# Routed experts on one core: parts of 16, 24 and 24 tiles, token rows scattered at other places, tile tables built sooner

## The chip, the core and the metric

One core of one Trainium2 chip runs the whole program. The metric is the device time of one execution in microseconds (us). TensorE (PE) multiplies and transposes, VectorE (DVE) and ScalarE (ACT) work on elements, GpSimd (POOL) does the same more slowly and issues the DMAs that need computed row numbers or an addition, and SyncE (SP) issues the plain DMAs.

## The reference

Tensors are float32. The input is 4 sequences of 2048 tokens with 256 channels, 8192 tokens in all.

```python
h = layernorm(x) * (1 + ca) + sa
x = x + ga * attention(h)            # 16 heads of 16, causal
h = layernorm(x) * (1 + cb) + sb
logits = h @ gate_w.T + bias         # 12 experts: 8 with weights, 4 that return h
top_w  = softmax(top 2 logits)
for e in the two chosen:
    y_e = silu(h @ w1[e].T) @ w2[e].T        # w1[e] 512 x 256, w2[e] 256 x 512
ffn = sum of top_w * y_e over chosen e < 8, plus (sum of top_w over chosen e >= 8) * h
x = x + gb * ffn
```

A token is computed only by the experts that it chose.

## The kernel before, in words

The program has three stages: attention, routing (`route`) and the experts (`experts`). The change touches the last two, and the sizes of buffers that attention clears.

**Parts.** The 64 tiles of 128 tokens are cut into three parts, `PARTS`. For each part there is a buffer `slot_x{p}` in HBM in which the rows of one expert lie together, each expert's rows rounded up to whole tiles of 128. A row holds the 256 channels of the normalised token and 6 numbers beside them (its place in `out`, its first expert, its two weights).

**Routing** runs over 16 blocks of 4 tiles as a hand-written pipeline. `blocks` (L1240) calls, in step s, each listed stage for block s - lag. DVE adds the attention output to `x` and takes the statistics (`residual`), ACT normalises into `hn`, POOL multiplies `hn` into `h2s` (`modulate`, L1734), DVE adds the shift into `h2` (`shifted`, L1600), PE transposes it and computes the logits, and DVE picks the two largest (`top2`). When all blocks of a part are through, DVE builds the one-hot choice (`chosen`, L1278 to L1285), PE counts with two matmuls (`counts`, L1319 and L1320), and DVE turns the counts into the row number of each token and choice (`placed`, first instruction L1327). Parts 0 and 2 have the lags 5 and 6, part 1 has lags of its own. After the pipeline DVE builds a table for each part (`tile_table`, L1360 to L1368): which expert each tile of the slot buffer belongs to (`eid`, `eidf`), where it changes (`turn`), and how many pairs of tiles there are (`npair`). The table uses the buffer of `hn` as scratch.

The pipeline also loads and transposes the weights of the 8 experts. `w_in` has two buffers for each of the two matrices; PE transposes each matrix in two halves (L1578), so 32 halves, each of which increments `wt_done`, and ACT copies them away. SP loads the next matrix (L1396, L1399) when a buffer has been transposed.

**Scatter.** `scatter_row` (L1376) is one indirect DMA on POOL: 128 rows of `h2` to their places in `slot_x{p}`, for one tile and one of its two choices, 134 KB. A tile has two of them, and a row DMA of a tile waits until that of three tiles earlier has landed. Part 0 is scattered during routing: three row DMAs in each of the last 8 blocks, the other 8 behind them. Parts 1 and 2 are scattered during the experts of the part before.

**Experts** go part by part, and in a part by pairs of tiles. For a tile, SP loads its 128 slots into `xs` (L1844), PE transposes it (L1870), multiplies with `w1` (L1878) and with `w2` (L1887), ACT copies `x_t` (L1919) and that expert's `w1` (L1923) and applies silu (L1915), DVE multiplies with the token's weight into `ys` (L1978, a ring of four buffers), and POOL adds it into `out` by an indirect DMA with addition (L2005). The buffer `ys[t % 4]` may be written again when the add of tile t - 4 has landed. An add waits for the add two tiles earlier, and where the expert changes (`turn`) for the one just before it, since the same token can be in both.

POOL's order in part p is written out (L2008 to L2026): pair i's two adds, then row DMAs of the next part until `due(p, i)` tiles are scattered, then in some pairs a zero term. A zero term (L1764 on DVE, the names `wc` and `zb` are one buffer; L1773 on POOL) adds the share of the four experts that return their input, for one group of four tiles; there are 16, and `ZTERMS` says in which part. SP may load the first tile of the next part once POOL has seen all its rows land and has incremented `x_ready`; this is checked once per pair, behind its adds.

Of the kernel before, what the change touches and what calls it, by code (L numbers as in the profile page):

```python
# [38 lines left out]
NB = NTOK // BLK  # L39
# [12 lines left out]
E, EZ, F = 8, 4, 512  # L52
# [3 lines left out]

PARTS = [16, 20, 28]
FIRST = [sum(PARTS[:p]) for p in range(len(PARTS))]
# [4 lines left out]
SCATTERING = 8  # L63
AHEAD = 0
NFILL = 12
# [6 lines left out]
GROUPS_OF = [list(range(FIRST[p] // TPB, (FIRST[p] + PARTS[p]) // TPB)) for p in range(NPARTS)]  # L72
ZTERMS = [GROUPS_OF[2], GROUPS_OF[0], GROUPS_OF[1]]
part_of = [p for p, n in enumerate(PARTS) for _ in range(n)]
XB = 4
# [1304 lines left out]
def scatter_tile(pool, d, r, t, scat):  # L1380

    for c in range(2):
        scatter_row(pool, d, r, t, c, scat)
# [37 lines left out]
def route(nc, a, d, k, r, w, w_in, w_ld, ps, out, scat, first, retired):  # L1421
    with ExitStack() as ctx:
# [35 lines left out]
        LASTS = [(FIRST[p] + PARTS[p]) // TPB - 1 for p in range(NPARTS)]  # L1458
        bank = ps[:, 7, :]

        with nc.Block() as block:
# [58 lines left out]
            def _(pe):  # L1520
# [60 lines left out]

                blocks((6, counts(0, 2)), (10, counts(1)), (0, output), (3, logits), (8, weights(0, 1)), (2, normed), (8, weights(1, E)))

            @block.vector
            def _(dve):
# [87 lines left out]
                def zeros(t):  # L1673
                    if t == LASTS[0]:
                        chains[0].zero_weights(dve, s, r)

                dve.memset(r["h2"][:, :, C:CE], 0.0).then_inc(ext_zero, 1)
                dve.wait_ge(ext_zero, 1)
                blocks((2, scales), (3, shifted), (5, top2), (0, attended), (1, residual), (4, inverses), (4, table),
                       (5, chosen(0, 2)), (6, placed(0, 2)), (7, zeros), (9, chosen(1)), (11, placed(1)))  # L1680
                dve.wait_ge(topi_done, NB)
                dve.wait_ge(mult_done, NB)
                for p in range(NPARTS):
                    tile_table(dve, s, r, p, cmp, eidf, last, turned)

            @block.scalar
            def _(act):
# [36 lines left out]

                blocks((1, deviation), (1, normalise), (5, shares(0, 2)), (10, shares(1)), (2, normed), (8, weights))

            @block.gpsimd
            def _(pool):
                def modulate(t):
                    pool.wait_ge(hn_done, t + 1)  # L1730
                    if t >= 1:
                        pool.wait_ge(mod_done, t)
                    apart(pool)
                    pool.tensor_tensor(h2s[:, :, :], hn[:, :, :], wide(k["sbc"][:, t // BPS, 1, None, :], 1, TPB), ALU.mult).then_inc(mult_done, 1)  # L1734

                todo = [(t, c) for t in range(PARTS[0] + AHEAD) for c in range(2)]

                def scatter():
                    t, c = todo.pop(0)
                    if (t, c) == (PARTS[0], 0):  # L1740
                        pool.wait_ge(pos_done, 4)
                    scatter_row(pool, d, r, t, c, scat[part_of[t]])

                def scatters(t):
                    if t >= NB - SCATTERING:
                        pool.wait_ge(pos_done, 2)
                        pool.wait_ge(mult_done, t + 1)
                        for _ in range(3):
                            scatter()

                blocks((0, modulate), (0, scatters))
                while todo:
                    scatter()
                scattered(pool, 0, scat[0])
# [21 lines left out]
def experts(nc, d, k, r, w, zb, ps, out, scat):  # L1776
# [3 lines left out]
    with ExitStack() as ctx:  # L1780
# [26 lines left out]
        ov = out.rearrange("b (n j p) c -> (b n) p j c", p=P, j=TPB)  # L1807
        later = [range(FIRST[p + 1] + (AHEAD if p == 0 else 0), FIRST[p + 1] + PARTS[p + 1]) if p + 1 < NPARTS else range(0) for p in range(NPARTS)]

        def due(p, i):  # L1810
            return len(later[p]) if i == NPAIR[p] - 1 else min(len(later[p]), -(-(i + 1) * len(later[p]) * 10 // (NPAIR[p] * 7)))

# [22 lines left out]
        with nc.Block() as block:  # L1835
# [157 lines left out]
            def _(pool):  # L1993
                for p in range(NPARTS):
                    def body(t, q, i):
                        pool.wait_ge(y_done[p], t + 1 + 2)
                        if t > 1:
                            pool.wait_ge(add_done[p][q], 16 * i)
                        if t in (1, 2):
                            pool.wait_ge(add_done[p][1 - q], 16)  # L2000
                        if t > 2:
                            turn = pool.value_load(r["turn"][0:1, p, t:t + 1], min_val=0, max_val=16)  # L2002
                            pool.wait_ge(add_done[p][1 - q], turn + 16 * ((t - 1) // 2))
                        apart(pool)
                        pool.indirect_dma_start(rows, bass.IndirectOffsetOnAxis(ap=idx[:, p, t:t + 1], axis=0), ys[:, t % YR, :], None,  # L2005
                                                compute_op=ALU.add).then_inc(add_done[p][q], 16)

                    used = tiles_used(pool, p)  # L2008
                    n, told = 0, not later[p]
                    for i in range(NPAIR[p]):  # L2010
                        pair(pool, i, used, body)
# [62 lines left out]
```

## Time and profile before

| | |
|---|---|
| median of 3 runs (lowest to highest) | 2663.47 us (2662.32 to 2663.79) |
| the profiled execution: time, and the span of its instructions | 2661.45 us, 2659.7 us |
| instructions | 48344 |
| PE busy, share of the span | 2484.9 us, 93% |
| DVE | 1904.5 us, 72% |
| ACT | 1668.7 us, 63% |
| POOL | 769.8 us, 29% |
| attention ends, routing begins | about 1970 us |
| experts begin | 2127.68 us |

Times in the rows below are microseconds from the start of the span. Busy time of an engine is time within its instructions; waiting, register and branch instructions are not in it. For an indirect DMA the record on POOL is the time in which POOL makes its descriptors, not that of the transfer. A bracket at the end of a row, `[2.10 <-PE ps L1887]`, is the idle time of that engine before the instruction, and what ended it.

### The profile page before, as it was taken

Reading aid. Unit: us, or ns where it says so; the run is one execution under the profiler, and the core shown is the slowest. Engines: PE = TensorE matmul, PEld = TensorE weight load, DVE = VectorE, ACT = ScalarE, POOL = GpSimd, SP = SyncE. Lnnn points to the kernel's source line nnn. Section 1 sums busy time; section 2 is a strip of 40 time slices with the busy share of each in tenths; the row PEclk is TensorE's granted clock in tenths of the full one; section 3 lists DMA queues with packets and bytes.
Section 4 is the critical chain, followed back from the end, with each engine's and each line's share of the span. In section 5 each row is a group of like instructions: output and inputs, shape, how many; then the busy total and the mean of one; then the engine's idle time right before and its main releaser. Section 6 shows DMA issues by size and latency. Waiting matters only on the chain. (4 is left out here: it accounts for less than half of the span.)

```text
span 2659.7 us, 48344 instructions
## 1 busy us (share of the span) xinstructions
PE 2484.9 (93%) x16082; PEld 1284.4 (48%) x16083; DVE 1904.5 (72%) x3227; ACT 1668.7 (63%) x2986; POOL 769.8 (29%) x895
## 2 busy tenths in 40 slices
PE   6987889999999999999999999999988798788998
PEld 3554233333333333333333333333347687678997
DVE  5987768788788788787787887887638644444654
ACT  2666357777777777777777777777764454344554
POOL 2545201121121111111111111111215467676443
PEclk8998789999999999999999999999999799899999
DMA  5798643252342442432432432320247656665653
GB/s 177 206 250 225 124 78 89 64 117 86 88 91 84 93 92 83 93 92 79 97 92 75 99 82 58 74 59 20 68 131 228 212 118 125 113 123 102 98 80 60
DMA packets 226331, 287.43 MB, mean 108 GB/s; under 512 B 29494, under 2 KB 179798, under 8 KB 225750
## 3 DMA queue, kind: packets, MB, share of 16 engines
q1 hardware_dynamic: 186988, 237.28, 35.1%
q0 software_dynamic: 32016, 41.44, 9.2%
q10 hardware_dynamic: 7136, 6.32, 0.7%
q8 instruction: 101, 1.65, 0.3%
q14 instruction: 90, 0.74, 0.1%
HBM read 143.51 MB, written 140.55 MB: 107 GB/s over the span
## 5 line engine op out<-in xcount | busy, mean ns | idle before, releaser
L238 DVE TENSOR_REDUCE mxc<-ps 128x2 f32<-128x1024 f32 (+4 forms) x1168 | 1298.1, 1149 | 316.0 <-PE ps L226 165.8
L1186 ACT ACTIVATE probs<-ps 128x512 f32<-128x512 f32 (+1 forms) x2240 | 1177.5, 587 | 462.0 <-PE ps L1143 450.4
L1159 PE MATMUL ps<-probs,vs 128*32 128x512 f32 (+3 forms) x5120 | 599.6, 541 | 1.3 <-POOL probs L1076 1.2
L1143 PE MATMUL ps<-qs,ks 99*128 99x512 bf16 (+3 forms) x1760 | 504.3, 352 | 13.9 <-DMA qs<-m_t 9.1
L226 PE MATMUL ps<-ks,qs 96*128 96x512 bf16 (+3 forms) x1760 | 464.4, 354 | 25.2 <-DVE mxc L238 17.4
L1076 POOL TENSOR_SCALAR_AFFINE_SELECT probs<-probs 128x512 f32<-128x512 f32 x256 | 162.4, 637 | 868.5 <-ACT probs L1186 868.4
L1143 PEld LDWEIGHTS ps<-qs,ks 99*128 99x128 bf16 x1760 | 147.5, 97 | 380.1 <-ACT probs L1186 271.8
L1878 PE MATMUL ps<-x_t,w_at 128*128 128x128 f32 x1984 | 250.1, 280 | 7.8 <-ACT w_at L1923 5.9
L2005 POOL DMA_INDIRECT out<-ys,idx x121 | 194.5, 1607 | 209.7 <-DMA out<-ys,idx 115.1
L226 PEld LDWEIGHTS ps<-ks,qs 96*128 96x128 bf16 x1760 | 163.4, 99 | 178.8 <-DVE mxc L238 42.4
L1878 PEld LDWEIGHTS ps<-x_t,w_at 128*128 128x128 f32 x1984 | 238.2, 196 | 10.3 <-ACT w_at L1923 7.9
L1887 PE MATMUL ps<-w2t,hid_t 128*128 x968 | 231.0, 382 | 6.8 <-ACT hid_t L1915 4.8
L1143 PE MATMUL ps<-shared 99*128 99x512 bf16 (+3 forms) x800 | 228.4, 349 | 0.0
L1159 PEld LDWEIGHTS ps<-probs,vs 128*32 128x32 f32 x5120 | 100.9, 108 | 228.8 <-issue 119.2
L226 PE MATMUL ps<-shared 96*128 96x512 bf16 (+3 forms) x800 | 207.8, 349 | 2.0 <-DVE mxc L238 1.8
L1978 DVE TENSOR_TENSOR ys<-ps,gm 128x256 f32<-128x256 f32 x121 | 51.4, 425 | 214.8 <-PE ps L1887 121.9
L1887 PEld LDWEIGHTS ps<-w2t,hid_t 128*128 128x128 f32 x968 | 175.4, 191 | 27.3 <-issue 8.2
L1923 ACT COPY w_at<-shared 128x1024 f32 x127 | 132.9, 1046 | 62.8 <-issue 56.2
L1919 ACT COPY x_t<-ps 128x256 f32<-128x256 f32 x127 | 47.2, 372 | 159.6 <-PE ps L1870 114.0
L1060 POOL CAST mparts<-negm 128x16 bf16<-128x16 f32 x64 | 12.6, 198 | 461.9 <-DVE negm L1205 461.9
L1143 PEld LDWEIGHTS ps<-shared 99*128 99x128 bf16 x800 | 66.9, 96 | 163.7 <-ACT probs L1186 118.2
L1376 POOL DMA_INDIRECT slot_x<-h,pos x128 | 132.1, 1032 | 43.0 <-issue 37.1
(172 smaller groups left out, 2220.5 us busy)
## 6 DMA issues: line engine op xcount, KB each, us to landing
ks<-k_parts SPq DMA_DIRECT2D x66, 256.0 KB, 4.1
qs<-q_parts SPq DMA_DIRECT2D x66, 256.0 KB, 4.1
xs<-slot_x SPq DMA_DIRECT2D x127, 131.0 KB
v_ones<-vout SPq DMA_DIRECT2D x64, 256.0 KB, 3.6
vs<-v_ones SPq DMA_DIRECT2D x64, 256.0 KB, 3.2
attn_t<-o_sb SPq DMA_DIRECT2D x64, 256.0 KB, 2.7
slot_x<-zero SPq DMA_DIRECT2D x36, 393.0 KB, 3.0
q_parts<-parts SPq DMA_DIRECT2D x96, 128.0 KB, 2.7
```

Source lines behind the costliest of these rows:

```text
L226: ins = pe.matmul(o[:, h, :], qs[0:SROWS, h0 + h, i * P:(i + 1) * P], ks[0:SROWS, h0 + h, 512 * c:512 * c + w], start=first, stop=not diag ...
L238: return dve.tensor_reduce(mxc[:, h0:h0 + nh, i, c], unit_view(ps, u, at), AX_X, ALU.max)
L1076: pool.affine_select(at, at, pattern=[[0, HG], [1, P]], base=0, channel_multiplier=-1, compare_op=ALU.is_ge, fill=keep).then_inc(mask_done, 1)
L1143: ins = pe.matmul(o[:, h, :], ks[r][0:SROWS + MROWS, h0 + h, j * P:(j + 1) * P], qs[r][0:SROWS + MROWS, h0 + h, J * QJ + lo:(J + 1) * QJ], ...
L1159: ins = pe.matmul(o_ps[SLOT * g:SLOT * (g + 1), lo:QJ], vs[:, r, j, SLOT * g:SLOT * (g + 1)], probs[:, (NKT * r + m) % NPB, g, 0:QJ - lo], ...
L1186: act.activation(probs[:, (NKT * r + m) % NPB, h0:h0 + nh, 0:QJ - lo], st_view(r, s), ACT.Exp, scale=DH ** -0.5).then_inc(exp_done, 1)
L1376: pool.indirect_dma_start(d[f"slot_x{p}"][:, :], bass.IndirectOffsetOnAxis(ap=r["pos"][c][:, t:t + 1], axis=0), r["h2"][:, t, :], None).th ...
L1878: ins = pe.matmul(ph[:, q, f * P:(f + 1) * P], w1_at[:, q, c, f * P:(f + 1) * P], x_t[:, q, c, :], start=(c == 0), stop=(c == KC - 1))
L1887: ins = pe.matmul(py[:, q, 0:C], h_t[:, q, f, :], w["w2t"][:, bass.ds(e, 1), f, :].rearrange("p o c -> p (o c)"), start=(f == 0), stop=(f ...
L1923: act.copy(w1_at[:, q, :, :], w["w1t"][:, bass.ds(e, 1), :, :].rearrange("p o c f -> p (o c) f")).then_inc(w1_done[p], 1)
L1978: dve.tensor_tensor(ys[:, t % YR, :], py[:, q, 0:C], gm[:, t % YR, :], ALU.mult).then_inc(y_done[p], 1)
L2005: pool.indirect_dma_start(rows, bass.IndirectOffsetOnAxis(ap=idx[:, p, t:t + 1], axis=0), ys[:, t % YR, :], None, compute_op=ALU.add).then ...
```

## The change

It cuts the parts otherwise, 16, 24 and 24 tiles in place of 16, 20 and 28. In routing, each of the last 8 blocks carries two row DMAs in place of three; of the other 16, the n-th (from 0) waits until 2n + 2 halves of weights are transposed. DVE builds the table of part 0 in step 17, that of part 1 in step 20, right behind `chosen` of part 2, and only that of part 2 at the end. In the experts, POOL scatters six tiles of part 1 (12 row DMAs) ahead of the first add, and the due times of the others follow another formula. Of the 16 zero terms, 2, 4 and 10 stand in the three parts, where it was 7, 4 and 5. The value of `turn` is loaded ahead of the waits of its add. `AT` makes the lags of part 1 follow from its last block; the steps come out as before (17, 18 and 19).

```diff
-PARTS = [16, 20, 28]
+PARTS = [16, 24, 24]
...
-AHEAD = 0
+EARLY = 6
...
-ZTERMS = [GROUPS_OF[2], GROUPS_OF[0], GROUPS_OF[1]]
+ZTERMS = [GROUPS_OF[2][:2], GROUPS_OF[2][2:], GROUPS_OF[0] + GROUPS_OF[1]]
...
+        AT = NB + 1 - LASTS[1]
...
-                blocks((6, counts(0, 2)), (10, counts(1)), (0, output), (3, logits), (8, weights(0, 1)), (2, normed), (8, weights(1, E)))
+                blocks((6, counts(0, 2)), (AT + 1, counts(1)), (0, output), (3, logits), (8, weights(0, 1)), (2, normed), (8, weights(1, E)))
...
+                def tables(p):
+                    def stage(t):
+                        if t == LASTS[p + 1]:
+                            dve.wait_ge(mult_done, NB)
+                            tile_table(dve, s, r, p, cmp, eidf, last, turned)
+                    return stage
+
...
-                       (5, chosen(0, 2)), (6, placed(0, 2)), (7, zeros), (9, chosen(1)), (11, placed(1)))
-                dve.wait_ge(topi_done, NB)
-                dve.wait_ge(mult_done, NB)
-                for p in range(NPARTS):
-                    tile_table(dve, s, r, p, cmp, eidf, last, turned)
+                       (5, chosen(0, 2)), (5, tables(1)), (6, placed(0, 2)), (7, zeros), (AT, chosen(1)),
+                       (AT, tables(0)), (AT + 2, placed(1)))
+                tile_table(dve, s, r, NPARTS - 1, cmp, eidf, last, turned)
...
                         pool.wait_ge(mult_done, t + 1)
-                        for _ in range(3):
+                        for _ in range(2):
                             scatter()
 
                 blocks((0, modulate), (0, scatters))
-                while todo:
+                for n in range(len(todo)):
+                    pool.wait_ge(wt_done, 2 * n + 2)
                     scatter()
                 scattered(pool, 0, scat[0])
...
         def due(p, i):
-            return len(later[p]) if i == NPAIR[p] - 1 else min(len(later[p]), -(-(i + 1) * len(later[p]) * 10 // (NPAIR[p] * 7)))
+            early = EARLY if p == 0 else 0
+            return min(len(later[p]), early - (-(i + 1) * (len(later[p]) - early) * 20 // (NPAIR[p] * 13)))
...
                     def body(t, q, i):
+                        if t > 2:
+                            turn = pool.value_load(r["turn"][0:1, p, t:t + 1], min_val=0, max_val=16)
                         pool.wait_ge(y_done[p], t + 1 + 2)
...
                         if t > 2:
-                            turn = pool.value_load(r["turn"][0:1, p, t:t + 1], min_val=0, max_val=16)
                             pool.wait_ge(add_done[p][1 - q], turn + 16 * ((t - 1) // 2))
...
                     n, told = 0, not later[p]
+                    if p == 0:
+                        while n < EARLY:
+                            scatter_tile(pool, d, r, later[0][n], scat[1])
+                            n += 1
```

POOL from the last block of routing to the first adds of the experts, before (`h2s` is the product of `modulate`, L1376 a row DMA, L2005 an add, L1773 a zero term):

```order
L1734 TENSOR_TENSOR h2s<-hn,sbc 128x1024
L1376 DMA slot_x<-h,pos 16640x262 x11
L1461 UNCONDITIONAL_BRANCH
L1992 UNCONDITIONAL_BRANCH
L1823 TENSOR_LOAD npair
L1823 ISA x2
L1823 TENSOR_LOAD npair
L1823 ISA x2
L1827 COMPARE_AND_BRANCH
L2005 DMA out<-ys,idx 8192x256
```

and now:

```order
L1740 TENSOR_TENSOR h2s<-hn,sbc 128x1024
L1376 DMA slot_x<-h,pos 15616x262 x18
L1462 UNCONDITIONAL_BRANCH
L1998 UNCONDITIONAL_BRANCH
L1829 TENSOR_LOAD npair
L1829 ISA x2
L1829 TENSOR_LOAD npair
L1829 ISA x2
L1376 DMA slot_x<-h,pos 15616x262 x12
L1833 COMPARE_AND_BRANCH
L2012 DMA out<-ys,idx 8192x256
```

Behind the last product stand 18 row DMAs in place of 11, the last 16 with waits for `wt_done`, and 12 more stand between the experts' begin and the first add.

DVE between the choice of part 2 (L1285) and its ranks (L1327), before:

```order
L1280 MEMSET c_flags 128x8
L1282 TENSOR_TENSOR c_oh<-c_idxf,iota_e 128x336 x2
L1285 TENSOR_TENSOR c_ohs<-c_oh 128x28x8
L1327 SCALAR_TENSOR_TENSOR c_cum<-c_flags,ps 128x224
L1328 TENSOR_SCALAR c_cnt_i<-c_cum 128x8
```

and now:

```order
L1285 TENSOR_TENSOR c_ohs<-c_oh 128x24x8
L1360 TENSOR_SCALAR last<-tend 128x1 x2
L1361 TENSOR_TENSOR hn<-tend,iota_t 128x464
L1362 CAST npair<-last 128x2
L1363 TENSOR_REDUCE eidf_all<-hn 128x58
L1364 TENSOR_SCALAR npair<-npair 128x2
L1365 TENSOR_TENSOR turned_at<-eidf_all 128x57
L1366 TENSOR_SCALAR turn<-turned_at 128x57
L1367 TENSOR_SCALAR eidf<-eidf_all 128x58
L1368 CAST eid<-eidf 128x58
L1327 SCALAR_TENSOR_TENSOR c_cum<-c_flags,ps 128x192
```

The table of part 1 has moved from behind everything to this place; that of part 0 stands the same way behind the choice of part 1.

## Rows read from the trace of the kernel before

**Rows 1.** Windows: us, busy of PE, PEld, DVE, ACT, POOL (instructions), PEclk, DMA share, GB/s

```profile
2131.00:2278.00 147.00, 123.31 (x831) 112.52 (x832) 60.60 (x263) 65.84 (x101) 98.78 (x78) 0.94 0.62 119
2454.00:2660.00 206.00, 194.32 (x1344) 181.01 (x1344) 108.14 (x436) 102.79 (x157) 89.61 (x57) 0.97 0.51 79
```

**Rows 2.** Timeline of DVE: part 1's first and last ys, part 2's last two

```profile
2284.88 0.42 DVE L1978 TENSOR_TENSOR ys<-ps,gm 128x256 f32<-128x256 f32 x1 [2.36 <-PE ps L1887]
...
2450.66 0.43 DVE L1978 TENSOR_TENSOR ys<-ps,gm 128x256 f32<-128x256 f32 x1 [1.56 <-PE ps L1887]
...
2645.10 0.42 DVE L1978 TENSOR_TENSOR ys<-ps,gm 128x256 f32<-128x256 f32 x1 [1.57 <-PE ps L1887]
2648.83 0.42 DVE L1978 TENSOR_TENSOR ys<-ps,gm 128x256 f32<-128x256 f32 x1 [1.57 <-PE ps L1887]
```

**Rows 3.** POOL's groups in 2131:2279, 2279:2455 and 2455:2660: count, busy, mean ns, idle

```profile
L2005 POOL DMA_INDIRECT out<-ys,idx x31 | 49.5, 1598 | 65.5 <-DVE ys L1978 39.5 <-DMA out<-ys,idx 18.7 <-issue 7.2
L1376 POOL DMA_INDIRECT slot_x<-h,pos x40 | 39.6, 991 | 12.2 <-issue 11.9 <-DMA out<-ys,idx 0.3
L1773 POOL DMA_DIRECT2D out<-wc x7 | 10.0, 1427 | 0.0
...
L2005 POOL DMA_INDIRECT out<-ys,idx x39 | 62.5, 1603 | 35.3 <-DMA out<-ys,idx 17.6 <-issue 9.4 <-DVE ys L1978 8.3
...
L2005 POOL DMA_INDIRECT out<-ys,idx x51 | 82.4, 1616 | 108.8 <-DMA out<-ys,idx 78.7 <-issue 18.1 <-DVE ys L1978 9.1
```

**Rows 4.** Chain that ended last, end of part 0: start, us, what

```profile
2260.57 5.00 DMA out<-ys,idx
...
2269.49 2.56 DMA slot_x<-h,pos
...
2272.10 3.48 DMA xs<-slot_x
```

**Rows 5.** Timeline of PE: first instruction of part 1

```profile
2275.71 0.66 PE L1870 MATMUL ps<-ident,xs 128*128 128x128 f32 x2 [17.11 <-DMA xs<-slot_x]
```

**Rows 6.** Timeline of POOL: last row in routing, first add, add of part 1's tile 34

```profile
2100.56 0.96 POOL L1376 DMA_INDIRECT slot_x<-h,pos  x1 [0.31 <-issue]
2139.79 1.62 POOL L2005 DMA_INDIRECT out<-ys,idx  x1 [38.27 <-DVE ys L1978]
...
2440.61 1.62 POOL L2005 DMA_INDIRECT out<-ys,idx  x1 [0.52 <-issue]
```

**Rows 7.** Timeline of DVE: ranks of parts 1 and 2, first instructions of the three tables

```profile
2103.33 0.49 DVE L1327 TENSOR_TENSOR_SCAN c_cum<-c_flags,ps 128x160 f32<-128x160 f32 x1 [9.08 <-remote]
...
2113.64 0.62 DVE L1327 TENSOR_TENSOR_SCAN c_cum<-c_flags,ps 128x224 f32<-128x224 f32 x1 [1.19 <-PE ps L1320]
...
2120.08 0.21 DVE L1360 TENSOR_SCALAR last<-tend 128x1 f32<-128x1 f32 x2
...
2122.18 0.21 DVE L1360 TENSOR_SCALAR last<-tend 128x1 f32<-128x1 f32 x2
...
2124.44 0.21 DVE L1360 TENSOR_SCALAR last<-tend 128x1 f32<-128x1 f32 x2
```

**Rows 8.** Timeline of SP: first load of a slot tile

```profile
2127.68 0.82 SPq L1844 DMA_DIRECT2D xs<-slot_x  x2
```

**Rows 9.** Timeline of PE: last transposes of weights

```profile
2120.03 1.09 PE L1578 MATMUL ps<-ident,w_in 128*128 128x128 f32 x8 [0.21 <-DMA w_in<-in_L_ffn_w]
```

**Rows 10.** Windows, as rows 1: the weights' loads

```profile
2104.00:2113.00 9.00, 6.71 (x36) 6.11 (x35) 7.62 (x47) 7.25 (x17) 0.00 (x0) 0.65 0.94 299
```

**Rows 11.** DMA, 2090 to 2100 us, POOL's queue: packets, MB, share of 16 engines

```profile
q0 software_dynamic: 415, 1.18, 32.3%
```

**Rows 12.** All row DMAs on POOL: duration ns, least, median and longest

```profile
L1376 POOL DMA_INDIRECT slot_x<-h,pos x128: 959/992/1929, 2032.1 to 2439.1; - x128
```

**Rows 13.** Chain that ended last, between the last ys and its add

```profile
2649.29 0.54 POOLq L2002
```

**Rows 14.** Timeline of PE: second count of part 1

```profile
2097.34 0.43 PE L1320 MATMUL ps<-c_ohs,ones 128*128 128x160 f32 x2
```

More of the change, by code:

```diff
@@ L1723, in weights @@
                         act.copy(dst, ps[:, half, :]).then_inc(wt_copy, 1)
-                blocks((1, deviation), (1, normalise), (5, shares(0, 2)), (10, shares(1)), (2, normed), (8, weights))
+                blocks((1, deviation), (1, normalise), (5, shares(0, 2)), (AT + 1, shares(1)), (2, normed), (8, weights))
             @block.gpsimd
@@ L1734, in modulate @@
                     pool.tensor_tensor(h2s[:, :, :], hn[:, :, :], wide(k["sbc"][:, t // BPS, 1, None, :], 1, TPB), ALU.mult).then_inc(mult_done, 1)
-                todo = [(t, c) for t in range(PARTS[0] + AHEAD) for c in range(2)]
+                todo = [(t, c) for t in range(PARTS[0]) for c in range(2)]
                 def scatter():
                     t, c = todo.pop(0)
-                    if (t, c) == (PARTS[0], 0):
-                        pool.wait_ge(pos_done, 4)
-                    scatter_row(pool, d, r, t, c, scat[part_of[t]])
+                    scatter_row(pool, d, r, t, c, scat[0])
                 def scatters(t):
@@ L1807, in experts @@
         ov = out.rearrange("b (n j p) c -> (b n) p j c", p=P, j=TPB)
-        later = [range(FIRST[p + 1] + (AHEAD if p == 0 else 0), FIRST[p + 1] + PARTS[p + 1]) if p + 1 < NPARTS else range(0) for p in range(NPARTS)]
+        later = [range(FIRST[p + 1], FIRST[p + 1] + PARTS[p + 1]) if p + 1 < NPARTS else range(0) for p in range(NPARTS)]
         def due(p, i):
-            return len(later[p]) if i == NPAIR[p] - 1 else min(len(later[p]), -(-(i + 1) * len(later[p]) * 10 // (NPAIR[p] * 7)))
+            early = EARLY if p == 0 else 0
+            return min(len(later[p]), early - (-(i + 1) * (len(later[p]) - early) * 20 // (NPAIR[p] * 13)))
         def z_from(p):
```

## The prediction

> **What bounds the kernel now.** I read the busy time by stage first, then the groups of POOL's instructions in each part, then the order of events at the seams.
>
> In the experts' first part TensorE is busy 123.31 us of 147, in the last 194.32 of 206 [rows 1]. So the parts have different limits. At the end of the last part two tiles' `ys` are 3.73 us apart [rows 2]; that is TensorE's own pace for one tile, and 51 tiles [rows 3] at 3.73 us are 190 us: the last part runs at it. The first two do not. In part 1, 39 tiles take from 2284.88 to 2450.66, 165.8 us [rows 2], where 38 steps of 3.73 us would be 141.7.
>
> What holds them is POOL [rows 3]. An add into `out` takes 1.60 us, a scattered row 0.99, a zero term's DMA 1.43, and 0.30 us of issue lies before each: 1.90, 1.29 and 1.73 us apart. In part 1 that is 39 x 1.90 + 56 x 1.29 + 4 x 1.73 = 153 us against TensorE's 142, and 17.6 us of waits for adds to land come on top. The ring of four `ys` passes POOL's lateness to VectorE and so to TensorE.
>
> The seam from part 0 to part 1 costs more. The add of tile 26 (pair 13) has to land, 5.00 us, because tile 27 is another expert's; then come the last rows of part 1, whose landing ends at 2272.05; only then may SP load the first tile of part 1 at 2272.10 [rows 4]. TensorE sat idle 17.11 us for that load [rows 5].
>
> Before the experts POOL is done with its rows at 2100.56 + 0.96 and has nothing to do until the first add at 2139.79 [rows 6]. Routing ends with VectorE: three tile tables, of which the first two take 2122.18 - 2120.08 = 2.10 and 2124.44 - 2122.18 = 2.26 us [rows 7], end at 2127, and the experts begin at 2127.68 [rows 8].
>
> **The change, part by part.** The tile counts come from the reference's own routing: for each part the (token, choice) pairs of each of the 8 experts, divided by 128 and rounded up. For 16, 20, 28 this gives 31, 39, 51, as the trace has it [rows 3]. For 16, 24, 24 it gives 31, 44, 45, which is 120: one tile less.
>
> *1. End of routing: -1.7 us.* Two scatters in place of three per block: the transfer of the last block's `h2s` to VectorE comes some 2.3 us sooner, but the table of part 0 (2.10 us) now stands there, ahead of the same add: nothing either way. The table of part 1 now stands between the choice of part 2 and its counts, where VectorE waits 1.19 us for TensorE anyway [rows 7]: it costs 2.26 - 1.19 = 1.07. So VectorE's end moves by -2.10 - 2.26 + 1.07 = -3.3 us; the wider part 1 and the narrower part 2 cancel (0.4 and 0.5 us, scaled from 20 and 28 columns).
>
> POOL's side is new. The 32nd row now waits for the last transpose, 2120.03 + 1.09 = 2121.1 [rows 9], and has to land, 2.56 us [rows 4]: 2123.9 with 0.2 of issue. Some 12 rows now lie beside the weights' loads, in a stretch where the DMA engines are busy 0.94 [rows 10]. Nine rows took 32.3% of 16 engines for 10 us, 0.36 us each [rows 11], so 12 are 4.3 us of DMA. I take a third of it as exposed: 2125.3. That is later than VectorE's 2123.7, so the beginning moves from 2127.68 to 2126.0. Bounds: -3.3 (VectorE's side) to +1.2 (all of 4.3 exposed).
>
> A row shows that a scatter beside VectorE's work may take up to 1.93 us in place of 0.96 [rows 12]. The Trainium skill (SBUF — State Buffer, "Who interferes with whom") speaks against the new place: VectorE's copies and tensor-scalar operations can lock the port through which GpSimd writes descriptors. By that rule the last row is up to 1 us later and this term is -0.7.
>
> *2. Part 0: -13.4 us.* The load of part 1 moves by four things. Its release no longer follows rows behind pair 13, since the new due times place all 24 tiles by pair 12: it comes when tile 26's add has landed, 2265.6 with 0.4 of issue in place of 2272.10, -6.1. Rows ahead of pair 13: 38 before, 48 - 12 = 36 now, -2.6. Zero terms: 7 before, 2 now, 5 x 1.73 = -8.6. And the 12 early rows, 12 x 1.29 = 15.5 us and 0.5 of decode, start at the experts' begin where POOL was idle for 12.1: the first add is 3.9 us later. Ends: -6.1 (only the release) and -17.1 (TensorE's whole idle time at the seam). I take the sum, as POOL stays 15 us behind TensorE's pace to pair 13 and so keeps every us it is given.
>
> *3. Part 1: +1.0 us.* Through the last pair with rows POOL took from 2284.88 + 1.2 to 2440.61 [rows 2, 6], 154.5 us, for 34 adds, 56 rows, 4 zero terms: 143.7 of work and 10.8 of waits. Now it is 38 adds, 48 rows, 4 zero terms: 141.0 and, with the same waits, 151.8, -2.7. Behind it six tiles in place of five follow at TensorE's pace, +3.7. Ends: -5.4 (43 x 3.73 = 160.4, no stall at all) and +11.8 (waits doubled).
>
> *4. Part 2: -22.4 us*, 6 tiles at 3.73. It gets ten zero terms in place of five. POOL idles 108.8 / 51 = 2.1 us ahead of each add there [rows 3]; 5 x 1.94 us hide in it, and would cost 9.7 if not.
>
> *5. The last add: -0.7 us.* The `turn` value is loaded before the wait for `ys`. At the end that load and what belongs to it took 0.54 us and some 0.2 behind it in the chain [rows 13]. Elsewhere it is hidden.
>
> Sum: -1.7 - 13.4 + 1.0 - 22.4 - 0.7 = -37.2 us. The profiled execution took 2661.45 us, so 2624.3; the median of the runs is 2.0 above it: **2626 us**. Attention, three quarters of the span, is not touched.
>
> **The rivals.**
>
> *TensorE binds from part 0 on (chance 0.20).* There are waits that no record of the trace ends: VectorE stood 9.08 us ahead of part 1's ranks with a release called "remote" [rows 7], though TensorE's counts were recorded as over by 2097.34 + 0.43 [rows 14], 5.6 us earlier, while POOL issued eight rows back to back. If such stalls come from bursts of rows, fewer bursts give 5 us in routing and the 5.4 of part 1, and the seam gives 2 more: 2626 - 12 = 2614. Against: the releases are inferred, and half of the bursts remain.
>
> *The early rows buy nothing (0.14).* The 12 rows hold the first adds, four `ys` fill, and the waits for landings grow with the tighter spacing. Then term 2 is only its release, -6.1, term 3 is +8: 2626 + 7 + 7 = 2640, to 2648 with the five zero terms exposed. For it: waits for `out` make 17.6 us in part 1 already [rows 3]. Against: POOL issues each add without a wait in most pairs.
>
> *Slower (0.04).* The rows now wait for the transposes, the transposes for the weights, and the weights share the DMA engines with the rows. If each of the 16 paced rows held the next load back by its own landing of 2.56 us, the begin would come 41 us late, and all the rest would be given back: 2626 + 41 + 2 = 2669. It decides at 37.2 / 16 = 2.3 us per row. Against: a row's measured share of the engines is 0.36 us [rows 11], and eight rows next to each other up to 2100.56 + 0.96 [rows 6] came 1.3 us apart. The Trainium skill (DMA: Bandwidth & Descriptors, "SWDGE vs HWDGE vs iDMA") says that software and hardware queues take turns in each engine, which is the mechanism of this rival; no row here shows turns that cost 2.3 us.
>
> **How the numbers follow.** The forecast has 0.62. Its own range, from the ends of its terms, is 2615 to 2637. With the first rival the low end is 2610, with the second the high end is 2645; about 2 in 10 lie outside. A measurement tells 0.2% (5.3 us) from no change. Faster by more: 0.62 + 0.20 + nearly all of 0.14, 0.94; within: 0.02; slower: 0.04.
>
> **What would show it.** Begin of the experts at 2126 (late: the weights' loads); first add 16 us behind it; TensorE's wait at the first seam 17.11 shrinking to 5 to 9; part 1 166.8 us from first `ys` to last, part 2 164 to 165; 31, 44, 45 adds. Wrong if the load of part 1 comes less than 6 us sooner after the begin, if VectorE waits for `out` in part 2, or if part 1 exceeds 172 us.

## The result, and the profile after

The changed kernel took 2636.21 us (median of 4 runs, 2635.21 to 2640.71), the kernel before on the same chip 2662.89 (4 runs, 2659.88 to 2663.79). The ratio is 0.9905, with a 95% interval of 0.9888 to 0.9922: faster, by 26.7 us of median where 37 were forecast (the two medians alone give 0.9900; the record's ratio is not taken from them). The time lies inside the range, 10 us above the forecast. The profiled execution has a span of 2635.3 us.

To compare stretch by stretch I cut each trace at five events of its timelines: the experts' begin (SP's first load of a slot tile), and VectorE's first and last `ys` of each part.

| us | before | after | difference | forecast |
|---|---|---|---|---|
| begin of the experts | 2127.68 | 2126.10 | -1.6 | -1.7 |
| begin to part 1's first `ys` | 157.2 | 151.0 | -6.2 | -13.4 |
| part 1, first to last `ys` | 165.8 | 170.5 | +4.7 | +1.0 |
| to part 2's first `ys` | 11.5 | 13.7 | +2.2 | 0 |
| part 2, first to last `ys` | 186.7 | 164.3 | -22.4 | -22.4 |
| last `ys` to the end | 10.9 | 9.7 | -1.2 | -0.7 |

So 24.4 us of span. Part 2 and the end gave what they should; what is missing lies in parts 0 and 1. The cuts come from these rows of VectorE's timeline of the changed kernel (start, us, engine, line, operation, idle time before it and what ended it), which answer to [rows 2]:

```profile
2146.75 0.42 DVE L1984 TENSOR_TENSOR ys<-ps,gm 128x256 f32<-128x256 f32 x1 [11.75 <-PE ps L1893]
...
2277.13 0.42 DVE L1984 TENSOR_TENSOR ys<-ps,gm 128x256 f32<-128x256 f32 x1 [1.90 <-PE ps L1893]
...
2447.59 0.42 DVE L1984 TENSOR_TENSOR ys<-ps,gm 128x256 f32<-128x256 f32 x1 [1.52 <-PE ps L1893]
2461.31 0.42 DVE L1984 TENSOR_TENSOR ys<-ps,gm 128x256 f32<-128x256 f32 x1 [4.16 <-PE ps L1893]
...
2621.88 0.43 DVE L1984 TENSOR_TENSOR ys<-ps,gm 128x256 f32<-128x256 f32 x1 [1.56 <-PE ps L1893]
2625.61 0.42 DVE L1984 TENSOR_TENSOR ys<-ps,gm 128x256 f32<-128x256 f32 x1 [1.56 <-PE ps L1893]
```

The first `ys` comes 20.6 us behind the begin; before it was 10.9. The chain of waits of the changed kernel, the profile's own account of what each step waited for, names the piece (start, us, what):

```profile
2126.10 3.12 DMA xs<-slot_x
2129.27 0.70 PE ps L1876 x2
2129.99 0.29 ACT x_t L1925
...
2131.97 1.28 ACT L1921
2133.26 8.84 another core or an unknown queue
2142.12 0.61 ACT hid_t L1921
```

ScalarE's first silu stood 8.84 us for a release that the profile can put to no recorded work. It needs the first tile's 16 matmuls into the hidden layer, and these are recorded as over long before:

```profile
2130.96 3.31 PE L1884 MATMUL ps<-x_t,w_at 128*128 128x128 f32 x16
...
2142.86 3.78 PE L1893 MATMUL ps<-w2t,hid_t 128*128 x8 [6.58 <-ACT hid_t L1921]
```

These two rows of TensorE's timeline show them over at 2134.27, 7.8 us before silu began at 2142.12; TensorE did the next tile's and then stood idle for silu, 6.58 us. "Another core or an unknown queue" ("remote" in the timelines) is the profile's name for a release that it cannot pair, and not a finding: in the semaphore records of the same trace the semaphore is one that TensorE's matmuls increment, and it rose at 2142.09. So it is TensorE's own increment that is recorded 7.8 us behind the recorded end of its matmuls. Those ends are modelled, so the trace does not tell whether the matmuls or only the increment came late. POOL meanwhile issued the 12 early rows one behind the other, of which the first and the last stand here with the first add (POOL's timeline, as [rows 6]):

```profile
2127.97 0.96 POOL L1376 DMA_INDIRECT slot_x<-h,pos  x1 [6.65 <-issue]
...
2141.91 0.96 POOL L1376 DMA_INDIRECT slot_x<-h,pos  x1 [0.30 <-issue]
2147.96 1.63 POOL L2012 DMA_INDIRECT out<-ys,idx  x1 [5.09 <-DVE ys L1984]
```

Silu began 0.2 us after the start of the last row. The stall is of the kind that [rows 7] hold, 9.08 us ahead of the ranks of part 1; that one is gone (now 3.38 us, for TensorE). Such waits make up 36.9 us of the engines' idle time between 2126 and 2266 in this trace and 40.7 between 2285 and 2450 (sums over VectorE and ScalarE, partly side by side). In the trace of before they are 27.4 and 41.8. All 56 of them, 28 in each trace, were ended by a semaphore of TensorE. Neither trace has one ahead of 2060 us or behind 2450 us, though part 2 is full of adds.

At the first seam SP issued the load of part 1 at 2260.63, 134.5 us behind the begin, where it was 144.4 before (2272.10, [rows 4]), 9.9 us sooner:

```profile
2260.63 0.82 SPq L1850 DMA_DIRECT2D xs<-slot_x  x2
```

So TensorE no longer waits for it, as it did in [rows 5]:

```profile
2268.46 0.41 PE L1876 MATMUL ps<-ident,xs 128*128 128x128 f32 x2 [2.36 <-issue]
```

POOL's groups in the stretches of [rows 3] (here 2131 to 2268 and 2445 to 2635 us; the second stretch also holds the last two adds of part 1):

```profile
L2012 POOL DMA_INDIRECT out<-ys,idx x31 | 49.9, 1610 | 26.9 <-issue 10.8 <-DVE ys L1984 8.7 <-DMA out<-ys,idx 7.4
...
L2012 POOL DMA_INDIRECT out<-ys,idx x47 | 75.6, 1609 | 94.7 <-DMA out<-ys,idx 51.8 <-DVE ys L1984 32.1 <-DVE wc L1769 6.1
L1778 POOL DMA_DIRECT2D out<-wc x10 | 18.5, 1853 | 0.5 <-issue 0.5
```

The ten zero terms of part 2 took 1.85 us each and cost nothing: 44 steps in 164.3 us are 3.73 each, TensorE's pace.

### The profile page after: what moved, and what is told of

Read it like the earlier page. It is cut to its first block and busy times, and to the rows that moved or that the text cites. A ratio compares the mean times of both kernels' runs of the same rounds, so it can differ in the third digit from the quotient of the medians.

```text
span 2635.3 us, 48256 instructions
## 1 busy us (share of the span) xinstructions
PE 2479.6 (94%) x16056; PEld 1281.0 (49%) x16057; DVE 1903.6 (72%) x3219; ACT 1668.2 (63%) x2983; POOL 764.4 (29%) x894
## 5 line engine op out<-in xcount | busy, mean ns | idle before, releaser
L1143 PEld LDWEIGHTS ps<-qs,ks 99*128 99x128 bf16 x1760 | 148.0, 97 | 378.9 <-ACT probs L1186 269.2
L1893 PE MATMUL ps<-w2t,hid_t 128*128 x960 | 230.3, 383 | 11.1 <-ACT hid_t L1921 8.3
L1893 PEld LDWEIGHTS ps<-w2t,hid_t 128*128 128x128 f32 x960 | 174.5, 192 | 32.4 <-issue 13.4
L1376 POOL DMA_INDIRECT slot_x<-h,pos x128 | 127.9, 999 | 60.7 <-issue 41.9
```

The lines of the kernel that those rows point to most:

```text
L1143: ins = pe.matmul(o[:, h, :], ks[r][0:SROWS + MROWS, h0 + h, j * P:(j + 1) * P], qs[r][0:SROWS + MROWS, h0 + h, J * QJ + lo:(J + 1) * QJ], ...
L1376: pool.indirect_dma_start(d[f"slot_x{p}"][:, :], bass.IndirectOffsetOnAxis(ap=r["pos"][c][:, t:t + 1], axis=0), r["h2"][:, t, :], None).th ...
L1893: ins = pe.matmul(py[:, q, 0:C], h_t[:, q, f, :], w["w2t"][:, bass.ds(e, 1), f, :].rearrange("p o c -> p (o c)"), start=(f == 0), stop=(f ...
```

## The experiments

Three questions were open. Does the burst of early rows itself make the stall of 8.8 us? Which edit brings what? And why is part 1 longer than forecast? The runs came in three jobs, on chips that the record numbers 10, 12 and 15 (the first result has no number). There the kernel before took 2646.7 to 2648.0 us (the three jobs' medians) and not 2662.9; I call them the other chips. So totals are compared by their ratio to the kernel before in the same job, and stretches within these twelve traces. Each kernel has one trace. The changed kernel has one on chip 12 and one on chip 15, and they differ by 2.9 us in the begin, 1.2 in the next stretch and 1.6 in part 1; a smaller difference between two traces means nothing by itself.

### The early rows, and what may stand in their place

Without early rows, all 48 rows of part 1 come between the adds:

```diff
-EARLY = 6
+EARLY = 0
```

> The changed kernel without the 12 early rows; the due times then spread all 24 tiles of part 1 over pairs 0 to 12. Theory A (the unbroken burst of 12 row DMAs holds back the other engines' semaphores: silu of the first tile started at 2142.1, 8 us after its matmuls, when the last row was being issued): the first ys comes 11 us behind the experts' begin, as before the change, in place of 20.6. Part 0 then carries 48 rows and gets longer (POOL bound: 12 rows x 1.29 = 15 us more), so from begin to the first ys of part 1 it is 155 to 160 us against 151, and the kernel about 2642. Theory B (the first ys is late for another reason, the slow TensorE clock or the silu table): first ys stays at +20, and the kernel is 2650 or more.

2630.21 us (4 runs), ratio 0.9932 [0.9916, 0.9949]. The first `ys` came 12.0 us behind the begin; to part 1's first `ys` it was 151.4 us. The 2642 us expected were for the first chip. And since no kernel shows the stall on these chips, a first `ys` without it, here and in the next two runs, says nothing about what makes it.

The same with 12 memsets on POOL in the rows' place, 13.94 us together, with no DMA:

```diff
-                            scatter_tile(pool, d, r, later[0][n], scat[1])
-                            n += 1
+                        for j in range(12):
+                            pool.memset(pace[:, :], 0.0).then_inc(pace_done, 1)
+                            pool.wait_ge(pace_done, j + 1)
```

> As the kernel without early rows, with 12 memsets of 128 x 1200 on POOL (about 1.1 us each, 14 us in all) where the early rows were, so that POOL is as busy but issues no DMA. It computes what the reference does. Theory A: first ys at +11, only the first add is late (+16). Theory C (POOL being busy is enough): first ys at +20.

2632.25 us (1 run). First `ys` at +12.0. The first add started 16.0 us behind the begin, 2.8 us later than without the memsets (13.2), and the total is 2.0 above, part 0 with its seam 1.9 (153.4). That would fit a price of what the first add is delayed, with the rest of POOL's time there free; but it is one run, and its time just outside the four of the run before (2627.39 to 2632.1), so it is not shown.

The 12 rows, each with a memset of 1.11 us behind it:

```diff
-                            scatter_tile(pool, d, r, later[0][n], scat[1])
+                            for c in range(2):
+                                scatter_row(pool, d, r, later[0][n], c, scat[1])
+                                pool.memset(pace[:, :], 0.0).then_inc(pace_done, 1)
+                                pool.wait_ge(pace_done, 2 * n + c + 1)
```

> The changed kernel with a memset of 128 x 1200 and a wait for it behind each early row, so that the 12 rows come 2.5 us apart in place of 1.27 and end 30 us behind the begin. Theory A (density of the burst): first ys within +11 to +14, first add at +31. Theory D (silu is held until the last early row, however sparse): first ys at +30. In both the kernel is slower than the changed one, since the ring of four ys fills.

2633.85 us (1 run). First `ys` at +12.0 again; the adds start so late that all the rows had gained is lost (part 0 129.9 us).

The change with the routing of before (three rows per block, the rest unpaced, all tables at the end), and the early rows as in the change:

```diff
-                        for _ in range(2):
+                        for _ in range(3):
...
-                for n in range(len(todo)):
-                    pool.wait_ge(wt_done, 2 * n + 2)
+                while todo:
```

> The changed kernel with the routing stage of before: three rows in each of the last 8 blocks, the other 8 unpaced, all three tables at the end. By the measured difference of the two begins (2127.7 and 2126.1) it is 1.5 to 3 us slower than the changed kernel, 2638 to 2639. Theory A: the wait called remote ahead of part 1's ranks is back (9 us, in place of 3.4), since eight rows are issued in one burst there. If the paced rows were what keeps the begin from coming sooner (last row issued at 2120.4, begin 2126.1), it could be equal.

2620.27 us (4 runs), ratio 0.9900 [0.9884, 0.9917]. This kernel has the full burst of 12 rows, and its first `ys` came at +11.0. None of the four traces has a single "remote" wait. The burst alone does not make the stall. The old routing was expected to cost 1.5 to 3 us, and its begin is the earliest of the job (2125.7). Against the run without early rows the ratio is 0.9932 - 0.9900 lower, some 8.5 us (9.9 by the medians): the early rows, with whatever the two routings differ by.

### The change again, and each part alone

> The change as it is, once more, on the chip of this job. Theory A (the burst of 12 row scatters at the experts' begin delays the releases of other engines): the first ys comes 20 to 21 us behind the begin, as in the first profile, with a wait of 8 to 9 us on ACT's first silu that no engine of the core ends. Theory C (these waits belonged to the chip or to that execution, not to the burst): first ys at +11 to +12, part 0 of 117 to 120 us, the seam behind it 11 to 12 us, part 1 163 us, part 2 164.3 us; ratio to the kernel before 0.989 to 0.991.

2619.8 us (4 runs), ratio 0.9894 [0.9877, 0.991]. First `ys` at +12.9, no stall. ScalarE's first silu waited 1.36 us, for TensorE. The same once more in the third job:

> The change as it is, on the chip of this job. Theory C (the waits that no engine ends belong to the chip): if the kernel before takes 2663 us here, they are in this trace too and the first ys comes 20 us behind the begin; if it takes 2648 us, there are none, the first ys comes at +11 to +13, and the span is about 2620. A 2648 us chip with such waits, or a 2663 us chip without, would speak against it. Ratio in both cases 0.989 to 0.991.

2619.52 us (4 runs), ratio 0.9894 again. ScalarE's timeline of that run, where the first chip had 8.86 us of "remote":

```profile
2133.72 1.28 ACT L1921 ACT_TABLE_LOAD   x1
2135.80 0.60 ACT L1921 ACTIVATE hid_t<-ps 128x512 f32<-128x512 f32 x1 [0.80 <-PE ps L1884]
```

VectorE's and TensorE's timelines of it, at the cuts:

```profile
2139.61 0.42 DVE L1984 TENSOR_TENSOR ys<-ps,gm 128x256 f32<-128x256 f32 x1 [2.89 <-PE ps L1893]
...
2269.10 0.42 DVE L1984 TENSOR_TENSOR ys<-ps,gm 128x256 f32<-128x256 f32 x1 [1.79 <-PE ps L1893]
...
2433.14 0.42 DVE L1984 TENSOR_TENSOR ys<-ps,gm 128x256 f32<-128x256 f32 x1 [0.55 <-PE ps L1893]
```

```profile
2260.35 0.66 PE L1876 MATMUL ps<-ident,xs 128*128 128x128 f32 x2 [7.09 <-DMA xs<-slot_x]
```

Here the seam looks as forecast: TensorE's 17 us for the load of part 1 are down to 7.09. The kernel before, profiled in the second job:

> The kernel before, for a profile on the same chip as the others of this job. Theory A and theory C alike: begin at 2127.7, first ys at +11, part 0 127 us, part 2 186.7 us. Theory C: the wait of 9.08 us of L1327 in the routing, which no engine of the core ended, is gone here too, and part 0, the seam or part 1 are shorter than in the first profile, since the same kernel takes 15 us less on another chip.

2650.32 us (1 run), span 2648.6. The 9.08 us of [rows 7] are 3.56 here, ended by TensorE, and TensorE's wait at the seam is what it was in [rows 5]:

```profile
2099.89 0.49 DVE L1327 TENSOR_TENSOR_SCAN c_cum<-c_flags,ps 128x160 f32<-128x160 f32 x1 [3.56 <-PE ps L1320]
```

```profile
2274.99 0.66 PE L1870 MATMUL ps<-ident,xs 128*128 128x128 f32 x2 [16.58 <-DMA xs<-slot_x]
```

Begin to part 1's first `ys` took 156.2 us (157.2 on the first chip), part 1 157.3 (165.8). None of the twelve traces of these jobs has a "remote" wait. They go with the first chip, or with that job; no second job on it tells the two apart.

The rows of part 1 scattered in the routing, between the weight transposes, in place of the burst at the begin:

```diff
-                todo = [(t, c) for t in range(PARTS[0]) for c in range(2)]
+                todo = [(t, c) for t in range(PARTS[0] + EARLY) for c in range(2)]
...
-                        for _ in range(2):
+                        for _ in range(3):
...
-                for n in range(len(todo)):
+                for n in range(8):
                     pool.wait_ge(wt_done, 2 * n + 2)
                     scatter()
+                pool.wait_ge(pos_done, 4)
+                for n in range(12):
+                    pool.wait_ge(wt_done, 18 + 14 * n // 12)
+                    scatter()
```

> The 12 rows of part 1 are scattered in the routing, between the weight transposes, and not at the begin; the experts start with n = 6 as before. Theory P (POOL is what part 0 waits for, so every row taken off it before the first add counts): begin within 1 us of 2126, the first add starts right behind the first ys, part 0 and the seam together 129 us or less, total 3 us below to 1 us above the change. Theory A: also 8 to 9 us below the change where that one shows the late first ys. Theory W (the rows in the routing delay the weight transposes or the begin): begin 3 us or more later, total equal to the change or above.

2615.2 us (4 runs), ratio 0.9882 [0.9865, 0.9898], the lowest of all. It stands 4.6 us below the change in the same job, more than the 3 us expected at most, though the intervals overlap. Part 0 took 112.8 us, 30 steps of TensorE's pace and 0.9 more. VectorE's group of `ys` from 2139 to 2258 us shows what had held it (first the change in the third job, then this kernel; count, busy, mean ns, idle time ahead and what ended it):

```profile
L1984 DVE TENSOR_TENSOR ys<-ps,gm 128x256 f32<-128x256 f32 x31 | 13.1, 424 | 66.5 <-DMA out<-ys,idx 47.9 <-PE ps L1893 18.4
```

```profile
L1988 DVE TENSOR_TENSOR ys<-ps,gm 128x256 f32<-128x256 f32 x31 | 13.2, 424 | 63.9 <-PE ps L1897 58.4 <-DMA out<-ys,idx 5.5
```

With the burst the four `ys` are full and VectorE waits 47.9 us for adds; without it 5.5.

The kernel before with the new parts alone:

```diff
-PARTS = [16, 20, 28]
+PARTS = [16, 24, 24]
...
-                blocks((6, counts(0, 2)), (10, counts(1)), (0, output), ...
+                blocks((6, counts(0, 2)), (9, counts(1)), (0, output), ...
```

> The kernel before with parts of 16, 24 and 24 tiles (and the blocks of part 1's tables put one step sooner, which 24 tiles ask for); routing and POOL's order as before, no early rows. Theory P: part 0 carries 48 rows of part 1 in place of 40, so part 0 with its seam is as in the run without early rows (139 us against 129.6 in the one with them), part 1 162 to 163 us, part 2 164.3 us: ratio 0.9932 as there, so the parts alone bring two thirds of the gain and the early rows the rest. Rival: the new routing has a share of its own, then this one stands 2 us or more above the run without early rows.

2637.12 us (6 runs), ratio 0.9961 [0.9949, 0.9974]: 10 us, little over a third of the gain and not two thirds. Begin to part 1's first `ys` takes 162.8 us against 151.4 in the run without early rows. I had put that run and this one equal and forgotten zero terms and due times. Two kernels split them.

### Zero terms, due times, and a better version

The change with six zero terms in part 0 (before had seven, the change has two):

```diff
-ZTERMS = [GROUPS_OF[2][:2], GROUPS_OF[2][2:], GROUPS_OF[0] + GROUPS_OF[1]]
+ZTERMS = [GROUPS_OF[2], GROUPS_OF[0], GROUPS_OF[1]]
```

> The change with the zero terms where they were: six in part 0 in place of two, four in part 1 as in the change, six in part 2 in place of ten. Theory P (POOL's work up to the release sets the load of part 1): part 0 and its seam together 4 x 1.73 = 6.9 us longer than in the change of this job, part 2 the same 164.3, total +7. Rival H (they fit where POOL waits for adds to land, 15 us in part 0): part 0 and seam +3 us or less.

2626.54 us (4 runs), ratio 0.9924 [0.9908, 0.9941], 7.0 us above the change of that job, as four zero terms at 1.73 us say. In the one profile the span is only 4.7 us longer: 5.6 between begin and part 1's first `ys` (147.0 against 141.4) and 1.2 in a later begin, less 1.3 in part 1 and 0.8 at the seam behind it. Part 2 takes 164.3 with six as with ten.

The change with the slope of the due times as before:

```diff
-            return min(len(later[p]), early - (-(i + 1) * (len(later[p]) - early) * 20 // (NPAIR[p] * 13)))
+            return min(len(later[p]), early - (-(i + 1) * (len(later[p]) - early) * 10 // (NPAIR[p] * 7)))
```

> The change with the slope of the due times as before (10/7 in place of 20/13 of the tiles per pair): the 24th tile of part 1 is placed by pair 13 and not by pair 12, so its release comes a pair later, behind the adds of pair 14. The step of the prediction said 6.1 us for this. Theory P: part 0 with its seam +4 to +6 us against the change, part 1 within 1 us. Rival: the release waits for the landing of the same add either way, then +2 us or less.

2619.9 us (4 runs), ratio 0.99 [0.9884, 0.9917]: nothing in the total (+0.4 us). The last row of part 1 starts at 2257.03 where the change has it at 2251.96, 5.1 us later; TensorE waits 11.59 us at the seam and not 7.09, and begin to part 1's first `ys` is 4.1 us longer, as theory P said. Part 1 is 2.6 us shorter (161.4), which it did not say. It looks as if part 1 gives back what the seam costs, but 2.6 us is not far above the 1.6 by which two traces of one kernel differ there.

Rows in the routing, and part 1's four zero terms in part 0:

```diff
-ZTERMS = [GROUPS_OF[2][:2], GROUPS_OF[2][2:], GROUPS_OF[0] + GROUPS_OF[1]]
+ZTERMS = [GROUPS_OF[2], [], GROUPS_OF[0] + GROUPS_OF[1]]
```

> Rows of part 1 in the routing as in the run of that name, and the four zero terms of part 1 put into part 0, so that POOL has none in part 1. There part 0 took 112.8 us, which is TensorE's own pace (30 x 3.73 = 111.9), with POOL waiting 18.6 us for ys; part 1 took 163.1 where TensorE's pace gives 160.4. Theory P: part 1 falls to 160.4 to 161.5, part 0 stays below 115, ratio to before 0.986 to 0.988. Rival: part 0 with its seam grows by 4 us or more, as POOL is needed there, and the total is equal to or above that run's 0.9882.

2621.89 us (4 runs), ratio 0.9912 [0.9895, 0.9928]: worse than the 0.9882 with rows in the routing alone. Part 1 came down to 160.6, its floor (43 steps of 3.73 us, 160.4), as theory P said, but begin to part 1's first `ys` rose from 137.2 to 142.8 us. The 18.6 us for which POOL had waited for `ys` lie nearly all in one wait, ahead of the first add, and can't take work that comes later.

The stretches side by side, us:

| kernel | begin | to part 1's first `ys` | part 1 | to part 2 | part 2 | span |
|---|---|---|---|---|---|---|
| before (second job) | 2127.6 | 156.2 | 157.3 | 11.1 | 185.5 | 2648.6 |
| new parts alone | 2125.5 | 162.8 | 162.0 | 12.6 | 164.4 | 2637.6 |
| change, no early rows | 2127.7 | 151.4 | 162.0 | 12.9 | 164.3 | 2628.1 |
| change (third job) | 2127.7 | 141.4 | 164.0 | 13.0 | 164.3 | 2620.1 |
| change (second job) | 2130.6 | 142.6 | 162.5 | 12.6 | 164.3 | 2622.0 |
| change, old routing | 2125.7 | 140.6 | 162.9 | 13.7 | 164.3 | 2616.9 |
| rows in the routing | 2126.8 | 137.2 | 163.1 | 13.3 | 164.3 | 2614.6 |

## Why the prediction was right, and where it was not

The mechanism held: POOL's work in part 0 sets the load of part 1, and the last part runs at TensorE's pace. The sum of -37.2 us was too large by 13 us of span on the first chip, by 9 to 11 on the other chips (2648.6 to 2620.1 and 2622.0). The range was not added up as it says: from the ends of its terms the high end is 2626 + 2.9 + 7.3 + 10.8 = 2647 and not 2637, the low end 2614. The time of 2636 is inside either. The terms in turn.

**Term 1, the end of routing (-1.7).** The profile after shows -1.6 with the begin at 2126.10, but this is no confirmation. The 9.08 us of [rows 7] were in the trace of before alone. From the start of routing (TensorE's first matmul of the attention's output) to the begin, before has 161.5 us on the first chip and 158.8 on chip 12; the new routing has 159.7 in the first profile and 159.0 to 163.1 in seven others with the paced rows of the change, mean 160.5 over the eight; the old routing with new parts has 158.0 and 157.3. The tables do end sooner, at 2119.3 and not at 2127.0, but the last row waits for the last transpose and starts at 2120.36; the begin follows 5.7 us behind it, its landing (2.56 us in [rows 4]) among them. If anything, the new routing costs some 2 us. The total can't tell: 0.9900 with the old routing, 0.9894 with the new, in different jobs.

**Term 2, part 0 (-13.4).** This is the step that failed on the first chip: -6.2. The sum of POOL's work had no row for a stall on ScalarE, and one of 8.84 us held the first `ys`. TensorE then took 119.5 us from the first `ys` to the last, where 30 steps are 111.9, waited 2.36 us at the seam and never for the load; the gain was there and could not be taken up. My sign of being wrong (the load of part 1 less than 6 us sooner behind the begin) did not show and did not catch this: the load came 9.9 us sooner (134.5 in place of 144.4), but TensorE's first matmul of part 1 only 5.7 (142.4 in place of 148.0), because TensorE was still busy with part 0. What the term had wrong is the path: it took POOL to be last to the end, and TensorE was. On the other chips, where the load came 14.2 and 14.7 us sooner, with no such stall, the term measures 141.4 - 156.2 = -14.8 and 142.6 - 156.2 = -13.6. So the arithmetic was right and its condition was not stated. Its parts, by pairs of kernels:

- New parts alone: +6.6 us (156.2 to 162.8), for eight more rows at 1.29 and one zero term less at 1.73, 8.6 by the prices in the sum.
- Zero terms: four of them 5.6 us in this stretch and 7.0 in the total, 6.9 by the sum.
- Due times: 4.1 where the earlier release was put at 6.1, and 0.4 in the total.
- Early rows: -10.0 and -8.8 us (151.4 to 141.4 and 142.6). The sum had 15.5 us of rows taken from between the adds, less 3.9 for the later first add, -11.6. Measured, the first add comes 17.2 us behind the begin in place of 13.2, 3.9 later. These two traces are from other jobs than the one without early rows.

Each size is 1.3 to 2.8 us off, and the errors cancel: that -14.8 and -13.6 stand so close to -13.4 is in part luck.

**Term 3, part 1 (+1.0).** +4.7 on the first chip, +5.2 and +6.7 on the others. The sum subtracted POOL's saved work from 165.8 us without asking how much of these was POOL's. 38 steps at 3.73 are 141.7; the kernel before stood 24.1 us above its floor on the first chip and 15.6 on chip 12. The new floor is 43 x 3.73 = 160.4. On chip 12 before took 157.3, so the sum would be 158.3, below that floor: the part runs into TensorE and ends at 162.5 and 164.0. That is the first rival's mechanism, in one part of three. What keeps it above is not shown: without zero terms it took 160.6, but with all four and slower due times 161.4. On the first chip part 1 stood 10.1 us above the floor, and its idle time has 40.7 us of "remote" releases.

**Seam to part 2 (nothing).** +2.2, and +1.5 to +1.9 on the other chips. In its three traces the changed kernel's TensorE waits 4.02 to 4.35 us there with no releaser that the profile shows ("issue"), in the first trace of before 2.32. The control instructions in the traces show what this is. `pairs` is a loop over `NPAIR` pairs, the most that the part can need, and behind the last pair that has tiles the engines still walk through the empty ones, three branches each. For 24 tiles `NPAIR` is 28 and 44 tiles use 22, so six are empty; for 20 tiles it is 24 and 39 tiles use 20, so four are. TensorE's sequencer moves on to a new pair with one MOVE (records of the loop's line ahead of the seam; first after, then before):

```profile
L1838 PEldq MOVE  x6: 29/29/29, 2445.5 to 2450.5; - x6
```

```profile
L1832 PEldq MOVE  x4: 29/29/29, 2448.8 to 2451.8; - x4
```

An empty pair takes it 1.0 us (the six MOVEs stand 5.0 us apart from first to last), and with two more of them the wait is 1.7 us longer, 4.04 in place of 2.32, most of the 2.2. All twelve traces with parts of 24 tiles have the six empty pairs and a wait of 4.01 us or more. The 2.36 us at the first seam are four empty pairs too. In the second trace of before, TensorE waits 4.58 us for the load of `xs` in that place. So a wider part has a price at its end that the sum had put at nothing.

**Terms 4 and 5.** Part 2 -22.4, exact; 21.2 on chip 12, whose trace of before had 1.2 less. The last add -1.2 and the like in all runs (9.5 to 9.9 us from the last `ys` to the end, 10.3 to 10.9 with the load of `turn` behind the wait); no run took this edit alone.

**The rivals.** "Remote" waits as the child of bursts: the run with the old routing has both bursts and none of the waits, so bursts are not enough. Whether they are needed on a chip that shows such waits was not tried, since none of the jobs met one again. "Early rows buy nothing": they buy 8 to 10 us of total, by runs that differ in routing or in job. "Slower by paced rows": the old routing in place of the new is worth nothing that can be measured, so a paced row costs far less than 2.3 us. The Trainium skill (SBUF — State Buffer, "Who interferes with whom") had spoken for a late last row by VectorE's hold on the shared port; in the trace the last row took 0.96 us, as little as the shortest of all 128, so the trace does not show it there.

That the chips give nearly the same ratio, 0.9905 and 0.9894, is partly luck: on the first chip the kernel before has 11 us more of span than on chip 12, and the changed one 13 to 15 more than on chips 12 and 15.

## What to carry to other kernels

- A busy engine's saved work is worth its price only down to the next engine's floor. Write that floor beside each stretch, and compare it with the stretch as it would be without the stalls of that one trace, before any saving is subtracted.
- Move work off a bound engine to where it is idle and nobody queues behind: the rows gain 8 to 10 us at the experts' begin, and some 4.6 more, by one pair of runs, between the weight transposes, where no add stands behind them. A large sum of idle time can be one wait that lies too early to help.
- A stall whose releaser the profile does not name may belong to the chip or the job. Take a second profile before it enters a sum or a theory.
- A wait that no semaphore ends can be control work. Look at the branches just ahead of it, and count the passes of a loop that have nothing to do.

## What was not expected of the hardware

The same kernel took 2662.9 us in one job and 2646.7 to 2648.0 in the next three, 0.6% apart, with the same granted clock (0.965) and equal attention (routing starts at 1966.2 and 1968.8 us). The difference of the spans, 11.1 us, and 2.6 more lie behind the routing's start: 2.7 us in the routing, 1.0 from the begin to part 1's first `ys`, 8.5 in part 1, 0.4 at the second seam, 1.2 in part 2. With it go the releases called "remote": up to 9.1 us each, on VectorE and ScalarE, only between 2099 and 2438 us, while POOL scatters rows (2032 to 2439). Every one is an increment by TensorE that is recorded at least 1.5 us behind the recorded end of its matmul. Part 2 has more adds per us (51 in 187, part 1 had 39 in 166) and none of them. Silu's came 7.8 us after its matmuls were over, with the end of the burst. On the other chips the same burst goes with no such wait. Why they were late on one chip is open.
